# In two slots of an attention pipeline, eight score reductions are issued in five heads instead of eight

## What is computed

```python
x = x + _layernorm(attn(_layernorm(x)))        # per row of 256 tokens, 16 heads
x = x + _layernorm(ffn(_layernorm(x)))         # shared + top-1 routed experts
# inside attn, for each row and head:
scores = jnp.einsum('bqhd,bkhd->bhqk', q, k) / np.sqrt(hd)
probs  = jax.nn.softmax(scores, axis=-1)
a      = jnp.einsum('bhqk,bkhd->bqhd', probs, v)
```

## Time and profile before

| | |
|---|---|
| median of three runs | 491.14 us (489.28 to 494.87) |
| profiled execution, own time | 493.12 us |
| its span, first to last instruction | 491.3 us |
| mean granted TensorE clock | 0.985 |
| PE busy | 443.4 us (90%) |
| DVE busy | 252.5 us (51%) |
| ACT busy | 185.5 us (38%) |
| POOL busy | 134.9 us (27%) |
| SM reductions, line 947 | 128, mean 686 ns |
| scores of SM, line 1308 | 256 matmuls, 10.1 us idle before them |

### The profile page before, as it was taken

How to read it: one execution, slowest core, us unless ns; L and a number is a source line. 1 busy time by engine, 2 the same in 40 slices (tenths; PEclk the granted TensorE clock), 3 DMA queues, 4 the chain that set the end, 5 groups by cost and what they waited for, 6 DMA issues and landing times.

```text
span 491.3 us, 7950 instructions
## 1 busy us (share of the span) xinstructions
PE 443.4 (90%) x2597; PEld 283.4 (58%) x2598; DVE 252.5 (51%) x591; ACT 185.5 (38%) x383; POOL 134.9 (27%) x195
## 2 busy tenths in 40 slices
PE   6888789999999997979899999999999999999691
PEld 5545456666666563636465665666666666655451
DVE  4454666868687857566767422222222222234765
ACT  2316557575757575555422122222222222211110
POOL 1214324343434424033020011111111110048533
PEclk9999999999999999989899999999999999999996
DMA  8772335353635363510575201111111111123311
GB/s 247 168 78 71 78 90 183 93 185 88 193 92 185 92 190 96 169 46 2 163 251 180 82 21 33 43 43 43 43 45 51 46 49 44 44 80 114 108 43 64
DMA packets 53990, 48.35 MB, mean 98 GB/s; under 512 B 5862, under 2 KB 49638, under 8 KB 53958
## 3 DMA queue, kind: packets, MB, share of 16 engines
q1 hardware_dynamic: 47424, 39.23, 27.8%
q0 software_dynamic: 1872, 5.11, 3.9%
q10 hardware_dynamic: 4662, 3.59, 2.6%
HBM read 25.78 MB, written 9.31 MB: 71 GB/s over the span
## 4 chain that ended last, share of the span: by engine, by line
PE 61%; DVE 15%; POOL 6%; issue 6%; DMA 4%; SPq 4%; ACT 2%; POOLq 0%; DVEq 0%; ACTq 0%
PE bank L1209 41%; PE bank L1213 7%; SPq L435 4%; DVE nmax L947 4%; PE bank L1344 3%; PE bank L1360 3%; PE bank L1308 3%; POOL pv L638 2%; PE bank L1284 1%; DMA x_sb<-x 1%; DMA stacks<-parts_q 1%; PE bank L1276 1%; DVE wall L977 1%; DVE stats_at L880 1%; POOL rstd_at L536 1%
## 5 line engine op out<-in xcount | busy, mean ns | idle before, releaser
L1209 PE MATMUL bank<-wall,stacks 128*128 (+2 forms) x616 | 212.9, 489 | 6.6 <-DVE stacks L1142 6.0
L1209 PEld LDWEIGHTS bank<-wall,stacks 128*128 128x128 f32 x616 | 111.4, 191 | 69.5 <-issue 59.6
L947 DVE TENSOR_REDUCE nmax<-bank 128x2 f32<-128x512 f32 x128 | 84.9, 686 | 51.0 <-PE bank L1308 50.8
L1138 DVE TENSOR_TENSOR stacks<-stacks,bank 128x512 f32<-128x512 f32 x39 | 26.8, 686 | 85.3 <-PE bank L1209 85.3
L1308 PE MATMUL bank<-stacks 96*128 96x256 bf16 x256 | 47.7, 273 | 10.1 <-DVE nmax L947 7.4
L622 POOL DMA_INDIRECT stacks<-x_sc,row_i x23 | 22.0, 955 | 124.3 <-PE bank L1213 124.3
L822 ACT ACTIVATE stacks<-bank 128x512 f32<-128x512 f32 x39 | 23.3, 597 | 81.7 <-PE bank L1209 81.7
L1142 DVE COPY stacks<-bank 128x512 f32<-128x512 f32 x39 | 26.9, 690 | 48.1 <-PE bank L1213 47.8
L1360 PE MATMUL bank<-stacks 99*128 99x256 bf16 x256 | 49.5, 276 | 1.9 <-ACT wall L784 1.6
L784 ACT ACTIVATE pv<-bank 128x512 f32<-128x512 f32 x64 | 37.9, 598 | 35.1 <-PE bank L1360 34.2
L784 ACT ACTIVATE wall<-bank 128x512 f32<-128x512 f32 x64 | 38.0, 603 | 31.6 <-PE bank L1360 30.7
(11 more groups left out here) (154 smaller groups left out, 529.8 us busy)
## 6 DMA issues: line engine op xcount, KB each, us to landing
wall<-gate_up SPq DMA_DIRECT2D x8, 1024.0 KB, 5.3
stacks<-parts_k SPq DMA_DIRECT2D x96, 64.0 KB, 2.6
stacks<-parts_q SPq DMA_DIRECT2D x91, 64.0 KB, 2.6
wall<-down SPq DMA_DIRECT2D x8, 512.0 KB, 6.4
y_exp<-stacks ACTq DMA_DIRECT2D x23, 128.0 KB, 1.7
x_tok<-wall SPq DMA_DIRECT2D x8, 256.0 KB, 2.6
stacks<-x_tok SPq DMA_DIRECT2D x16, 128.0 KB, 2.3
out<-stacks SPq DMA_DIRECT2D x8, 256.0 KB, 2.2
```

What stands on the lines that cost most here:

```text
L947: dve.tensor_reduce(nmax[:, half, qt, 2 * pair:2 * pair + 2], two(sm_bank[u % 2]), AX.X, ALU.max, negate=True).then_inc(sm["sm_max"], 1)
L1138: dve.tensor_tensor(hid, sg, fu[:, :], ALU.mult).then_inc(sm["h_sb"], 1)
L1209: last = pe.matmul(out_ap, lhsT, rhs, start=(n == 0), stop=(n == len(pairs) - 1))
```

## The change

The function that gives the units of each head gets a case for the slots 5 and 6. Up to head 7 nothing changes. Then units 8 and 9 stand at head 8, 10 and 11 at head 9, 12 and 13 at head 10, unit 14 at head 11 and unit 15 at head 12; heads 13 to 15 have none. Slot 7, which the condition covers too, takes no units at all. The matmuls, the reductions and all waits are the same in number and kind.

```diff
-            if not (isinstance(b, int) and b == 0):
+            if b >= B - 3:
+
+                return {8: ((1, 8), (1, 9)), 9: ((1, 10), (1, 11)), 10: ((1, 12), (1, 13)), 11: ((1, 14),),
+                        12: ((1, 15),)}.get(h, ((1, h),) if h < 8 else ())
+            if b:
                 return ((1, h),)
             if h < 4:
                 return (0, 2 * h + 8), (0, 2 * h + 9)
```

## The result

The changed kernel ran 20 times at a median of 494.73 us (492.84 to 499.17), the kernel before beside it 20 times at 493.06 (489.28 to 497.24). The ratio is 1.0049, 95% interval 1.0026 to 1.0071: **slower by 0.49%, some 2.4 us**. The forecast was +1.2 us. The time lies in the range, but half of the loss was missed; part of that is a step of the sum. The profiled execution took 492.8 us of span (494.56 of time), against 491.3 (493.12).

The account below looks back on a forecast made before the run. Bound: two chains ending at the slot's boundary, the reductions and the D chain from D_wo. Terms −0.1 (delays against a removed clock fall) and +1.3 (new fall) gave +1.2 on 491.14, so 492.3 us; range 489.3 to 495.3.

Parts of the forecast that it names:

- D_wo later by 0.69: Slot 5, heads 8 to 10: D_wo moves from 183.41 to 184.10, +0.69 us, by VectorE's bound; ScalarE's alone gives +0.44.
- M1 held by the D chain, not by the reductions: Slot 6, head 2: M1 follows D_power2 on GpSimd, so early reductions can't help and slot 6 runs 0.69 us late.
- the second ends 0.47 us later: At the slot's boundary: of two chains, reductions and D chain from D_wo, the D chain ends 0.47 us later.
- The won time waited away at head 0 for M0's transfer: Slot 6, head 0: the 1.3 us won are lost to a new wait of about 1.6 us for M0's transfer.
- The second wait: Slot 6, before M1 at head 2: the wait of 0.47 us grows to over 1, elsewhere given as 2.1 us.
- Slot 7 held by E_xn2: Start of slot 7: E_xn2 on VectorE, behind D_power2, ends at 218.86 instead of 217.48, and E_xn2T waits for it.
- The 1.38 us vanish in this execution: −0.1: Into slot 7: two D_wo delays, 1.38 us, offset by losing the clock fall at 214, some 1.4 us; D_avT0 −0.1.
- the fall at slot 6: Start of slot 6: thin work between new waits lets the clock fall, +1.3 us, bounds 0 and 1.5.
- The carrying to the median: Whole kernel: the difference of +1.2 us from the profiled execution goes unchanged to the median of three, 491.14 us.
- the two clock terms, −1.4 and +1.3: Fall at 214 before slot 7 removed, some 1.4 us back; new fall at slot 6's start, 1.3 us lost.
- The rule of the Trainium skill: Start of slot 6: rival that the clock stays up, fall term 0, sum −0.1, 491.0 us; chance 0.16.

Follow-up runs that it names:

- the filled pair: Changed kernel and kernel before, each with extra unused matmuls in its waits at the boundaries; ratios to the kernel before 0.9985 and 0.9996.
- the changed kernel again: The changed kernel run once more, unchanged, beside the kernel before; six runs, median 497.93 us, ratio 1.0111.
- slot 6 alone: The new order of units in slot 6 only, slot 5 as in the kernel before; median 493.07 us, ratio 1.0002.
- filled old waits: Kernel before with 12 and 16 unused matmuls ahead of units 14 and 15 in slots 5 and 6; median 491.57 us, ratio 0.9996.
- D_y first in slots 5 and 6: Kernel before with D_y ahead of unit 11's reduction on VectorE in slots 5 and 6; 488.46 us (0.9912), run again 489.65 us (0.9943).

## Why the prediction was right and where it was wrong

**D_wo later by 0.69:** right, 0.71 in slot 5 and again in slot 6 (4.19 against 3.48), with both bounds in their places. **M1 held by the D chain, not by the reductions:** right; shown from both sides, by delaying D_wo alone and by taking M1 out from behind D_power2. But "the second ends 0.47 us later" misreads: the 0.47 us are TensorE's wait for M1, not the distance of the two chains. VectorE's row of the kernel before shows the last reduction of the half, the first of these two, and D_power2 ends at 193.05+0.71 = 193.76:

```profile
192.88 1.28 DVE L947 TENSOR_REDUCE nmax<-bank 128x2 f32<-128x512 f32 x2
```

With the 0.69 us of one reduction it ends at about 193.57, some 0.2 us before D_power2. Both chains were nearly equal; in the changed kernel the reductions end almost 4 us earlier and the D chain alone is left.

**The won time waited away at head 0 for M0's transfer:** right, 1.30 us where I said 1.6. The second wait, for which I said over 1 in one place and 2.1 in another, was 0.62 for a reduction and 0.85 for M1. **Slot 7 held by E_xn2:** right, with 1.56 us of wait for it. Without low clock the prediction comes to 1.3 for both boundaries (the −0.1 plus the 1.4 that it gave the clock); the filled pair shows 1.19.

**"The 1.38 us vanish in this execution: −0.1":** right for the two profiles, -0.28 (1.19 minus the 1.47 that the low clock at 214 had cost); the changed kernel has 1.00 there, and so have the other two profiles in which slot 6 has the new order and VectorE and GpSimd keep theirs (the changed kernel again, slot 6 alone).

**The failed step is the fall at slot 6, "I take a fall, and 1.3, as part of it will lie in the wait".** The fall came, in both profiles of the changed kernel, but it measured 2.08 in the first and 2.16 in the second (25.57-23.41). I had taken one stretch of the length seen at 214, minus cover. It lasted 6.8 us, some 1.6 of them in waits and the rest over E_xn2T, three heads and a quad. Where the same waits were followed by 3.4 us only (slot 5 changed alone), the cost was 1.50, near the term: the length was wrong, not the mechanism. With 2.08 in its place the sum is -0.28+2.08 = +1.8. That is the difference of the two profiles from head 8 to slot 7's M1 (42.37 against 40.55) by the way it is made up, so it confirms nothing by itself; the medians of 20 differ by 1.67, the ratio gives 2.4 with an interval from 1.3 to 3.5.

**The carrying to the median was unsound** even so, and it is the other part of the missing loss. In the forecast the two clock terms, −1.4 and +1.3, cancel; in the runs they don't, since 2.4 us are some 1.2 more than the clean 1.19. The 1.47 taken off belong to one execution. In four of six boundaries with the old order the clock fell, so on average the credit may hold, or not: filled old waits gained 0.2 us, with 1.5 us at the edge of the interval. I also carried it to a median of three runs, 491.14, that twenty put at 493.06. What stays open is the rest of the pooled difference, 3.55 us against 1.8: longer or more low stretches in executions without a trace would explain it (one version's trace has 13.6 us of low clock in slot 6), but none of them was traced. Such stretches also lie away from the two boundaries: the changed kernel's profile has one of 3.4 us near 51 and another near 459, the kernel before's has neither. How often they come in either kernel isn't known.

The rule of the Trainium skill (page "TensorE: Matmul & The Clock Gate", section "Why this matters for your kernels") to avoid single long idle gaps would have given no fall at all. At the start of slot 6 no wait was above 1.30 us and the clock was low for 6.8 us; with the waits filled it stayed at 1.00. The trace does not agree with the rule as a bound.

## What to carry to other kernels

Before work is brought forward, look at what its consumer stands behind in its own engine's order: eight reductions finished almost 4 us early were worth nothing behind D_power2, and swapping two steps in one engine's order was worth more than the whole rearrangement. When a stall is removed and the same path has another holder, the idle time isn't removed but gathered elsewhere, and gathered idle time can cost the clock. And one profile shows one draw of the clock: the clean cost came out to 0.1 us, the clock's share only by filling the waits.

## What the runs showed of the hardware

The clock fell in some executions and not in others at one and the same code: at slot 6's start the unchanged order had 1.00 in the kernel before and 0.50 from 196 to 199 in the kernel with slot 6 changed alone. The low stretches at the boundaries were 3.4, 6.8 or 13.6 us long, the shortest and the longest of them at the same place of one kernel (D_y first in slots 5 and 6). On the distance from head 8 to head 8, each against the nearest trace without low clock, the three lengths cost 1.50 to 1.57, 2.08 to 2.16 and 5.03 us. A low stretch goes on though TensorE is busy: 2.89 us of the 3 from 196 to 199 in the changed kernel, and in the longest one 3.00, 3.00, 2.90 and 3.00 from 196 to 208, at clocks of 0.50, 0.50, 0.50 and 0.62. One of these windows:

```profile
199.00:202.00 3.00, 3.00 (x15) 2.20 (x14) 1.32 (x3) 1.46 (x4) 0.00 (x0) 0.50 0.92 318
```

With 20 short matmuls of useless work in each of three waits the clock was 1.00 at both boundaries, and the median 2.6 us lower.
